# A memset of a dead buffer in front of each of the 880 gathers of a two-layer graph kernel

## What is computed

```python
# layer 0: graph attention
h = (relu(layernorm(x)) @ W.T)                       # (3125, 8, 16)
e = a_src[src] + a_dst[dst];  e = where(e >= 0, e, 0.2 * e)
p = exp(e - segment_max(e, dst)[dst])
x = x + segment_sum(p / denom[dst] * h[src], dst) + bias
# layer 1: transformer-like attention with edge attributes
q, k, v = h @ Wq + bq, h @ Wk + bk, h @ Wv + bv      # h = relu(layernorm(x))
score = sum(q[dst] * k[src]) / 4 + edge_attr @ We + be
out = segment_sum(softmax(score) * v[src], dst) @ Wo + bo
x = x + layernorm(out + h) * gamma + beta
```

## Time and profile before

| | |
|---|---|
| median of 3 runs | 1561.81 us (1560.83 to 1562.72) |
| span of the profiled execution | 1585.9 us |
| TensorE's mean granted clock | 0.666 |
| TensorE busy | 1020.5 us, 64% |
| VectorE busy | 934.6 us, 59% |
| GpSimd busy | 883.4 us, 56% |
| ScalarE busy | 640.0 us, 40% |
| DMA queues | 110.35 MB, mean 70 GB/s |

### The profile page before, as it was taken

The page is one execution under the profiler, slowest core; times in us unless marked ns, Lnnn a source line. Parts: engine busy times, 40 slices in busy tenths (PEclk is TensorE's granted clock), DMA queues, the critical chain, the costliest instruction groups (busy, mean ns, idle before and its releaser), DMA issues.

```text
span 1585.9 us, 21105 instructions
## 1 busy us (share of the span) xinstructions
PE 1020.5 (64%) x4985; PEld 863.7 (54%) x4985; DVE 934.6 (59%) x3002; ACT 640.0 (40%) x1699; POOL 883.4 (56%) x926
## 2 busy tenths in 40 slices
PE   5456666666665766666554577666766676676765
PEld 4345555555554555445354466565655566566664
DVE  6445656556565565557813455656565656656578
ACT  5524334243342433422554234444443434344414
POOL 5766666666666566551046566656666565666500
PEclk9655555555656565566766666877777777777676
DMA  6321222222222222222133222222222222232201
GB/s 138 72 66 43 66 46 66 48 63 45 67 47 67 45 65 47 58 84 57 49 94 95 73 84 84 84 80 80 84 84 84 80 82 81 84 88 83 80 1 41
DMA packets 54202, 110.35 MB, mean 70 GB/s; under 512 B 16876, under 2 KB 30848, under 8 KB 53956
## 3 DMA queue, kind: packets, MB, share of 16 engines
q0 software_dynamic: 36288, 91.12, 22.6%
q1 hardware_dynamic: 16483, 17.39, 4.0%
q10 hardware_dynamic: 1313, 0.50, 0.1%
HBM read 100.60 MB, written 8.81 MB: 69 GB/s over the span
## 4 chain that ended last, share of the span: by engine, by line
DVE 16%; PE 16%; another core or an unknown queue 10%; issue 9%; ACT 2%; DVEq 2%
PE bank L865 6%; PE bank L849 6%; DVE acc L1441 4%; DVE PV L1418 3%; DVE prod L1238 2%; PE bank L836 1%; PE bank L912 1%; DVE raw L1247 1%; DVE halves L1087 1%; PE bank L900 1%; DVEq L1441 1%; ACT S L636 1%; DVEq L1220 0%; DVEq L90 0%
## 5 line engine op out<-in xcount | busy, mean ns | idle before, releaser
L532 POOL DMA_INDIRECT G<-table,idx_all x880 | 857.1, 974 | 544.5 <-issue 280.3
L865 PE MATMUL bank<-PV,S 128*125 128x144 f32 x1760 | 449.5, 416 | 209.5 <-DVE acc L1441 104.4
L865 PEld LDWEIGHTS bank<-PV,S 128*125 128x125 f32 x1760 | 373.9, 287 | 236.1 <-issue 134.9
L1441 DVE TENSOR_TENSOR acc<-acc,bank 125x144 f32 x880 | 260.4, 296 | 339.3 <-remote 191.7
L636 ACT ACTIVATE S<-iota_n,lid 128x125 f32<-128x125 f32 x880 | 275.7, 386 | 0.7 <-issue 0.7
L849 PE MATMUL bank<-qe,ST 125*128 x880 | 182.0, 378 | 87.3 <-DVE prod L1238 80.7
L849 PEld LDWEIGHTS bank<-qe,ST 125*128 125x128 f32 x880 | 164.1, 279 | 96.7 <-issue 95.8
L1418 DVE TENSOR_TENSOR PV<-G,PV 128x512 f32<-128x512 f32 x220 | 151.2, 688 | 23.4 <-issue 22.8
L646 ACT ACTIVATE ST<-bank 125x512 f32<-125x512 f32 x110 | 63.6, 598 | 248.4 <-remote 197.6
L640 ACT ACTIVATE S<-S,ones 128x500 f32<-128x500 f32 x220 | 156.6, 712 | 7.3
L836 PE MATMUL bank<-ident,S 128*125 128x128 f32 x440 | 89.8, 340 | 52.5 <-ACT S L640 31.9
(11 more groups left out here) (219 smaller groups left out, 1093.8 us busy)
## 6 DMA issues: line engine op xcount, KB each, us to landing
G<-table,idx_all POOLq DMA_INDIRECT x880
prod<-in_edge_attr_dram SPq DMA_DIRECT2D x8, 672.0 KB
table<-G SPq DMA_DIRECT2D x12, 224.0 KB
bias_rows<-qe SPq DMA_DIRECT2D x1, 1664.0 KB
table<-h0b SPq DMA_DIRECT2D x8, 178.5 KB
out_dram<-G SPq DMA_DIRECT2D x8, 168.0 KB
prod<-in_edge_attr_dram SPq DMA_DIRECT2D x8, 90.0 KB
xs<-in_x_dram SPq DMA_DIRECT2D x1, 504.0 KB
```

Of the source, the lines that this page charges most:

```text
L532: pool.indirect_dma_start(G[:, u, v, 0:w], None, table, bass.IndirectOffsetOnAxis(ap=idx_all[:, g * GV + v:g * GV + v + 1], axis=0)).then_ ...
L865: last = pe.matmul(sums_bank(p)[0:BN, at:at + H * SLOT], S[:, ur, v, :], PV[:, v, :, :].rearrange("p h k -> p (h k)"), start=True, stop=True)
L1441: ve.tensor_tensor(a, a, o, ALU.add).then_inc(s.sem["acc_added"], 1)
```

## The change

A function `space` issues a memset of the whole of `w0n` and counts it in a semaphore of its own; each memset waits for the count of the one before. `gathers` calls it in front of each of the 880 gathers, behind `pace`. The waits of `pace` and for `pv_ready` remain.

```diff
+        s_space = sem("spacer_set")
...
+            spaces = [0]
+
+            def space():
+
+                wait(pool, s_space, spaces[0])
+                pool.memset(w0n[:, :], 0.0).then_inc(s_space, 1)
+                spaces[0] += 1
+
             def gathers(n, table, w):
...
                         for v in range(QV * j, QV * j + QV):
                             pace(n, g, v)
+                            space()
                             pool.indirect_dma_start(
```

## The result

The changed kernel took 1620.53 us (median of 4 runs, 1607.32 to 1629.67), the kernel before 1562.26 us (1560.83 to 1564.03) on the same chip. The ratio is 1.036, 95% interval 1.030 to 1.042. The forecast was 1478 us, the wrong side by far, and the time lies above the range. The profiled execution of the changed kernel is the fastest of its four (1607.32 us, span 1605.6 us), and the one of before (span 1585.9 us) lay above its median; so the two traces differ by 20 us, and the rest of the 58 us is in no trace.

The account below looks back on a forecast made before the run. Bound: a backlog of gathers, served in 1.39 us but issued each 1.25, holding TensorE's counts. 1585.9 - 34 - 50 + 1 = 1503 us profiled, less 24 is 1479; forecast 1478 us, 8-in-10 range 1440 to 1590.

Parts of the forecast that it names:

- The reading of the bound: GpSimd's gathers: issued each 1.25 us but served in 1.39, their backlog holds TensorE's counts and causes pauses of about 2.5 us.
- TensorE's modelled ends: TensorE's counts: rival that they only look late because ends are modelled too early, so nothing changes, 1563 to 1565 us; chance 0.08.
- I take 0.17: GpSimd between two gathers: a memset adds 0.17 us, bounds 0 to 0.34, making the pitch 1.42 us.
- the forecast's condition: GpSimd's gather stream: its pitch, put at 1.42 us, must exceed the 1.39 us service so that the backlog stops growing.
- half the effect: GpSimd's gathers: rival that a memset adds 0.05 to 0.12 us and the backlog still grows, 1520 to 1550 us; chance 0.12.
- the law: TensorE's late counts: they come 0.56 us plus 1.39 us for each gather behind a run's first gather.
- The sum: Time of a group: 24.74 us for two runs of eight before; 23.7 us after, saving 34 and 50 us in the layers.
- counts only come when a run is over: TensorE's counts: rival that gathers in flight hold them until the last lands, 25 us lost, 1587 us; chance 0.15.
- some waiting: Each group: 1.0 us for waiting left and a lower TensorE clock, added to 22.7 us of gathers, giving 23.7.
- a lower granted clock: TensorE: with less idle time it may be granted less than 0.57 and 0.74; counted within 1.0 us a group.
- The rule of the Trainium skill: DMA against TensorE: DMA never contends with compute engines, so gathers could not hold TensorE; the forecast went against it.

Follow-up runs that it names:

- e2: The changed kernel with its memset widened from 128 to 290 columns in front of every gather: 1529.86 us, ratio 0.964 to the kernel before.
- e10: The changed kernel with its memset widened to 290 columns, a repeat of e2 on another chip: 1500.70 us, ratio 0.960 to the kernel before.
- e3: The changed kernel with two memsets of 290 columns in front of each gather instead of one of 128: 1829.30 us, ratio 1.154 to the kernel before.
- e7: The kernel before plus a one-column memset in front of every fourth gather only, taking over the waits: 1623.18 us, ratio 1.040.
- e1: The changed kernel with its memset shortened from 128 columns to 1: 1654.15 us, ratio 1.042 to the kernel before.
- e9: The changed kernel, GpSimd in layer 0 waiting for `hop1` at visit 8 instead of 12, its `scoreT` wait dropped: 1630.59 us, ratio 1.038 to the kernel before.
- e4: The kernel before, no memset, with `pace` waiting for TensorE's counts only at visit 0 of a group: 1834.33 us, ratio 1.156.
- e5: The changed kernel with its memset widened from 128 to 230 columns: 1535.29 us, ratio 0.980 to the kernel before.
- e14: The kernel of e7 with its one-column memset in front of the waits, which stay on the gathers: 1568.47 us, ratio 1.003 to the kernel before.
- e12: The kernel before, with gathers fetching 64 rows instead of 128 from the fourth group of each layer on: 1608.07 us, ratio 1.030.

## Why the prediction was wrong

**The reading of the bound was right.** TensorE's counts are held by a backlog of gathers that comes to 1.39 us each, the pauses are its working off, and GpSimd's stream becomes the limit once its pitch is over that: e2, e10 and e3 show it, and with 290 columns in place of 128 the kernel is 4% faster than before the change. The late counts are not TensorE's modelled ends: the very product that was 8.2 us late after the change is 0.04 us late in e10.

**The first step that failed is the price of a memset, "I take 0.17".** It measured 0.08, inside the range of 0 to 0.34 but less than half of what I took. I had the row for its length (0.19 to 0.21) and the 0.30 us of idle time ahead of a gather, and named only the extreme of the overlap. The memset takes its time out of that idle time until 0.16 us of it is left. One column (0.11 us) is free, 128 add 0.08, 230 add 0.17 and 290 add 0.22. With 1.33 against 1.39 the forecast's condition wasn't met, and the margin on which I had built was 0.03 us. The prediction said itself "by little" and went on as if it were enough.

**The second is what happens below the threshold.** My rival *half the effect* had just this price, "x is 0.05 to 0.12", and gave it 1520 to 1550 us. That didn't follow even from the law: as long as runs are of eight and the pitch is under 1.39 us, a group is 2 x (0.56 + 8 x 1.39 + 0.69) = 24.74 us at any pitch, and nothing is gained; nor do groups of 24.0 to 24.7 us give that range (by the forecast's own sum they give some 1495 to 1530). The sum took each run as eight gathers long. But a pause is ended by a count and begun by one that isn't there yet; when the counts come a little sooner against GpSimd's visits, GpSimd finds them at visit 8 and goes on, and the run becomes twelve or sixteen. The law, linear in the length, makes that no dearer for GpSimd: 0.56 + 0.69 us is even spared. It can be dear for the others: a count computed in the middle of the run waits for the whole backlog, up to 8 us, and the carry (`hop1`, `hop2`, the scans, ScalarE's exponent) needs several such counts one after the other. That the new pattern is dear is shown for layer 1 of e7 and e1. In layer 0 it is only argued. ScalarE's wait for DD, which belongs to layer 0, went from 191.2 us (L673, before) to this:

```profile
ACT EP L683 <- DVE DD L1392: 300.0, 29, 13.6
```

But it doesn't measure the loss: it is 296.0 us in e7, whose layer 0 is hardly longer, 92.3 in e9 and 165.3 in e4, both slow.

The rival *counts only come when a run is over*, slower by 25 us, also kept its runs of eight and is refuted by e10; it had the sign and not the cause.

**The third is the size of the gain above the threshold.** With the price as forecast (e5, pitch 1.42) the ratio is 0.980, and not 1478 / 1561.81 = 0.946. Its stretches are these:

```profile
108.00:660.00 552.00, 377.07 (x1730) 298.64 (x1730) 336.45 (x1090) 222.97 (x619) 475.77 (x731) 0.56 0.24 58
850.00:1400.00 550.00, 381.20 (x1975) 340.27 (x1974) 336.46 (x1036) 232.80 (x616) 466.89 (x717) 0.73 0.30 86
```

731 and 717 instructions are 22.8 and 22.4 groups, 24.2 and 24.5 us each where 23.7 was forecast. Single gathers last 1.1 to 1.6 us, so that the mean is 0.99 and not the 0.95 of the sum, which is 0.7 us a group, and with 0.03 us of margin some pauses come back, most in layer 1. The 1.0 us of "some waiting" stood for all that lies above 16 x 1.42 = 22.7 us, and 1.5 and 1.8 us were needed. It also stood for a lower granted clock, which e5 shows hardly (0.56 and 0.73, before 0.57 and 0.74) and e10 not at all.

**The rule of the Trainium skill** (SBUF — State Buffer, Who interferes with whom), by which TensorE never waits on anyone, would, as I read it, have made the added time a loss. The sign came out so, but not for that reason: 290 columns take more of GpSimd's time than 128, and win. Of matmuls the rule may hold; for when their counts rise it does not, in any trace here.

**What stays open.** What makes the changed kernel lose in layer 0, where most of its runs of sixteen cost nothing and six groups of 24 are 3 us dearer. Why a one-column memset that takes the waits (e7) breaks the pattern of eights and the same memset ahead of them (e14) doesn't. In both a gather starts about 0.7 us after the count. In the group shown of e7 the run's first gather lasted 1.65 us instead of 0.94 and the count for visit 8 came in time; that is one instance and no cause. What serves the gathers is open too: e12 excludes rows and bytes. That longer runs cost time is shown by e4, where only waits were taken away, and for layer 1 by the groups of e7 and e1; for layer 0 of the changed kernel it isn't shown.

## What to carry to other kernels

When a wait is not for data but orders two streams, look at what the pause that it makes lets through, before touching anything near it: four loops that meet through counts settle into a pattern, and an edit that costs nothing by itself can throw them into another. Near a threshold, price the edit against its margin. A forecast that needs 0.14 us and gets it from a term with bounds of 0 and 0.34 is a coin toss, and the time on the wrong side must be worked out anew with the new order of events, not as a part of the gain. And check the cost of a wait against the time of the group that it stands in: the late `hop1` shown above stood in a group that took no longer than before, and ScalarE's wait for DD was a third of the changed kernel's in e9, which lost as much.

## What the runs showed of the hardware

TensorE's semaphore counts come late while GpSimd issues indirect gathers closer than about 1.4 us apart: 8.2 us behind the product in a run of sixteen at 1.33 us, 5.9 us in one of twelve at 1.25 us, 0.04 us at 1.47 us. Behind a run's first gather at 1.25 us they come after 11.66 us for eight (86 counts, before), 17.19 for twelve (46, e4; both are medians) and 22.7 to 23.0 for sixteen (14 of 24 in e4, the others sooner). It doesn't go by the amount gathered (128 or 64 rows). A GpSimd memset over 128 partitions took 0.11 us for 1 column, 0.22 for 128, 0.31 for 230 and 0.36 for 290, and ran into 0.14 us of the idle time ahead of a gather. In e10's stretches TensorE's granted clock was 0.61 and 0.78 where the earlier trace rows had 0.57 and 0.74; over the whole program it was 0.694, but 0.652 in e2, the same kernel on another chip, and 0.666 before. With it went the remote waits that were left, 9.9 us in e10 and 98.2 us in e2. Which of the two comes first the runs don't tell. Of the 29 us between their profiled executions 18 lie behind the last gather (64.4 us to the end in e10, 82.5 in e2).
